# Fewer, larger transfers through a new row layout, and a new order of the stages of each quad, in a fused attention and ternary feed-forward kernel

## The chip, the cores and the metric

One core of one Trainium2 chip runs the whole kernel. The metric is the device time of one execution in microseconds (us). Everything stated of the hardware below comes from one profiled execution of the kernel before and from three timed ones.

## The reference, cut to what matters

```python
x = x + layernorm(attention(layernorm(x)))            # x: 8 x 1024 x 256, float32
x = x + layernorm(layernorm(x) @ (ternary(W) * alpha).T + bias)

# attention: 16 heads of 16, clipped relative positions (64 each way)
logits = einsum('bhqd,bhkd->bhqk', q, k) + einsum('bhqd,qkd->bhqk', q, embK[idx])
w      = softmax(logits)
out    = einsum('bhqk,bhkd->bhqd', w, v) + einsum('bhqk,qkd->bhqd', w, embV[idx])
return out @ Wo.T + bo

# ternary: delta = 0.7 * mean|w|;  +1 above delta, -1 below -delta, else 0
```

The mask is all ones and isn't used. The softmax subtracts the row's largest logit.

## The kernel before, in words

The work is 128 **steps**: 8 batches, 2 groups of 8 heads each, 8 query tiles of 128 tokens. Four steps are a **quad**, so a batch is four quads. A quad's slots in the planner's table are 32 long.

Queries and keys are split into three bfloat16 parts, and a logit is the sum of six products of parts over the 16 channels, which is one contraction over 96 rows. To these rows come two rows that carry minus the row's maximum (`MAXROW`) and three that carry the relative term of far keys (`FAR`): 101 rows in the tiles `qs` (queries) and `ks` (keys). The parts travel through DRAM (`qd`, `kd`), since each channel has to move to another partition: `write_q`, `write_k` and `write_far` (L643, L713) store them, `load_q`, `load_k` (L772, L722) bring them back in rows. A second, smaller copy for the row maxima, `mqs` and `mks` (48 main rows and 3 far rows, two heads on two halves of the partitions), comes by `load_mq` and `load_mk` (L751, L731).

One step issues on TensorE (the planner's stage names, with the letters used below):

- `row_max` (S, L919): main products of the *next* steps' queries into one of three banks `scores`; VectorE reduces each to a maximum (L1216, L1222).
- `max_rows` (L929): turns the maxima; SyncE moves them into `qs` (`max_move`, L812).
- `band_raw` (L902): the relative logits of near keys against `bandtab`; ScalarE copies them to `praw` (L1403, L1404), SyncE writes them skewed to DRAM `bs` (`band_write`, L785) and reads them back as `bands` (`band_read`, L798).
- `weights`: logits of one key tile for four heads, in one of two banks `logitsT`. A **plain block** (P) is four matmuls (L946). A **near block** (N), two of the eight per head group, adds four matmuls of `bands` (L946 and L950 in turn). ScalarE takes the exponential of each block out of its bank (L1424) into `wl`, `wm`, `wr` or `wy`. A step has 16 blocks. A block waits on `exp_ready` until its bank, that of the block before the last, was read.
- `weighted` (V): weights times values into `oacc` (L970), in kind X (the first four key tiles) and Y (the other four).
- once a quad: `relative` (L982), `relative_sum` (L995), `out_norm` (L1006); once a tile of the second group the **tail**: `tail_attT`, `tail_x1T` (L1020), `tail_wo`, `tail_ff` (L1034), with VectorE and GpSimd around them; once per two tiles of the next batch the **chunk**: `turn_x` (L865), `project_q`/`project_k` (L875), `far` (L883), `project_v` (L892).

The order of all of it is not written as code. `PLACES` (L109 to L169) gives each stage a slot within its quad, `LAG` and `END_LAG` shift a stage on one engine, `HOLD` says how long a stage keeps one of the two `misc` banks; `timetable()` lays the slots out, `with_banks` puts off what finds no bank, `order_of` sorts each engine's stages by slot. Engines then run these lists with semaphore waits. Four of TensorE's slots per half step are `near` (the blocks X0 to X3), four `rest` (Y0 to Y3). SyncE issues all DMAs, in its list's order.

The start of the program is special: batch 0's four chunks (256 tokens each) are projected, stored and loaded before the first step; in front of the list come constant loads (L656 to L661), fills of constant rows by DMA from a tile `junk` (L668, L672) and from zeros (L677). `load_table` (L689, L692) brings the tables of the later stages, at slots -33.2 on. `ternary` (L856 and VectorE) makes the ternary weight from `wf`.

## Time and profile before

| what | value |
|---|---|
| timed runs | 2567.48, 2572.11, 2575.16 us, median 2572.11 |
| profiled execution, span from first to last instruction | 2568.1 us |
| profiled execution, its own time | not listed beside the span |
| mean granted TensorE clock | 0.979 of full speed |
| TensorE matmul busy (PE) | 2413.4 us, 94% |
| VectorE busy (DVE) | 2072.1 us, 81% |
| ScalarE busy (ACT) | 1564.0 us, 61% |
| GpSimd busy (POOL) | 955.9 us, 37% |
| DMA queue of SyncE | 695686 packets, 427.75 MB, 60.8% of 16 engines' span |

PE is TensorE's matmuls, PEld its weight loads, which overlap them. A window row gives busy time with the number of instructions for each engine, then the granted clock, the DMA engines' busy share and GB/s. A timeline row gives the start, the length, and in brackets the idle time in front of it with what ended it; several equal instructions in a row are one row with a count. A row of SPq is a DMA issue on SyncE's queue: its length is the time of issuing, not of the transfer.

### The profile page before, as it was taken

Reading aid. Unit: us, or ns where it says so; the run is one execution under the profiler, and the core shown is the slowest. Engines: PE = TensorE matmul, PEld = TensorE weight load, DVE = VectorE, ACT = ScalarE, POOL = GpSimd, SP = SyncE. Lnnn points to the kernel's source line nnn. Section 1 sums busy time; section 2 is a strip of 40 time slices with the busy share of each in tenths; the row PEclk is TensorE's granted clock in tenths of the full one; section 3 lists DMA queues with packets and bytes.
Section 4 is the critical chain, followed back from the end, with each engine's and each line's share of the span. In section 5 each row is a group of like instructions: output and inputs, shape, how many; then the busy total and the mean of one; then the engine's idle time right before and its main releaser. Section 6 shows DMA issues by size and latency. Waiting matters only on the chain.

```text
span 2568.1 us, 101028 instructions
## 1 busy us (share of the span) xinstructions
PE 2413.4 (94%) x41858; PEld 1747.5 (68%) x41858; DVE 2072.1 (81%) x5306; ACT 1564.0 (61%) x2993; POOL 955.9 (37%) x2211
## 2 busy tenths in 40 slices
PE   5499999999999999999999999999999999999995
PEld 4266776777766776767776677676776777676673
DVE  4477779877888878887788878987788877888876
ACT  2266666666666666666666666666666666666651
POOL 3001534435343354425444253433534335442024
PEclk8599999999999999999999999999999999999998
DMA  6856675666746576565756667566774657756510
GB/s 162 228 155 180 184 195 146 167 176 193 205 138 174 165 205 185 148 193 152 206 153 176 184 182 194 147 168 174 199 201 139 173 163 203 192 145 189 153 42 29
DMA packets 696145, 434.20 MB, mean 169 GB/s; under 512 B 215846, under 2 KB 695430, under 8 KB 695558
## 3 DMA queue, kind: packets, MB, share of 16 engines
q1 hardware_dynamic: 695686, 427.75, 60.8%
q8 instruction: 329, 5.39, 0.9%
q14 instruction: 130, 1.06, 0.1%
HBM read 231.91 MB, written 194.92 MB: 166 GB/s over the span
## 4 chain that ended last, share of the span: by engine, by line
PE 54%; DVE 13%; issue 4%; ACT 3%; POOL 1%; DMA 0%; SPq 0%; DVEq 0%; ACTq 0%; POOLq 0%
PE logitsT L946 13%; PE oacc L970 12%; PE scores L919 7%; PE logitsT L950 6%; DVE junk L1222 4%; DVE maxes L1216 4%; PE misc L1034 3%; PE misc L875 3%; PE misc L995 2%; PE misc L892 2%; PE misc L902 1%; ACT wr L1424 1%; PE misc L982 1%; DVE stats L1092 1%; PE misc L1006 1%
## 5 line engine op out<-in xcount | busy, mean ns | idle before, releaser
L946 PE MATMUL logitsT<-qs,ks 98*128 98x128 bf16 (+1 forms) x8192 | 915.7, 221 | 21.8 <-ACT wr L1424 8.8
L1222 DVE CUSTOM_DVE_ANT_1 junk<-scores,bands 128x512 bf16<-128x512 f32 x988 | 679.5, 688 | 216.1 <-PE scores L919 66.7
L1424 ACT ACTIVATE wy<-logitsT 128x512 f32<-128x512 f32 x1024 | 581.4, 597 | 332.3 <-PE logitsT L946 321.1
L946 PEld LDWEIGHTS logitsT<-qs,ks 98*128 98x128 bf16 (+1 forms) x8192 | 562.4, 99 | 274.9 <-issue 150.4
L1216 DVE TENSOR_REDUCE maxes<-scores 128x1 f32<-128x512 f32 x1024 | 656.5, 682 | 93.8 <-PE scores L919 92.5
L919 PE MATMUL scores<-mks,mqs 48*128 48x256 bf16 (+6 forms) x3712 | 448.5, 289 | 36.8 <-DVE maxes L1216 12.6
L1424 ACT ACTIVATE wr<-logitsT 128x512 f32<-128x512 f32 x512 | 305.3, 596 | 200.2 <-PE logitsT L946 191.6
L950 PE MATMUL logitsT<-ident,bands 128*128 128x128 f32 x2048 | 410.6, 278 | 0.0
L1453 POOL TENSOR_SCALAR rs<-rs 128x1 int32<-128x1 int32 (+1 forms) x217 | 48.6, 224 | 803.3 <-DVE rs L1097 793.8
L950 PEld LDWEIGHTS logitsT<-ident,bands 128*128 128x128 f32 x2048 | 293.2, 143 | 20.6
L1458 POOL TENSOR_SCALAR rs<-rs 128x1 f32<-128x1 f32 x744 | 282.7, 383 | 64.9
L970 PE MATMUL oacc<-wy,vs 128*17 128x128 f32 (+1 forms) x9216 | 275.2, 262 | 4.5 <-ACT wy L1424 4.0
L919 PEld LDWEIGHTS scores<-mks,mqs 48*128 48x128 bf16 (+1 forms) x3712 | 138.9, 94 | 196.9 <-DVE maxes L1222 30.2
L1424 ACT ACTIVATE wl<-logitsT 128x512 f32<-128x512 f32 x256 | 158.6, 619 | 154.3 <-PE logitsT L950 152.5
L1463 POOL TENSOR_SCALAR rs<-rs 128x1 f32<-128x1 f32 x744 | 219.6, 298 | 66.1
L970 PEld LDWEIGHTS oacc<-wy,vs 128*17 128x17 f32 x9216 | 206.2, 97 | 53.1 <-issue 34.7
L1403 ACT ACTIVATE praw<-misc 128x512 f32<-128x512 f32 x256 | 154.7, 604 | 40.3 <-DMA bs<-praw 32.5
L1245 DVE COPY_PREDICATED wm<-later,wl 128x512 f32<-128x512 int32 x224 | 171.1, 764 | 0.0
L1424 ACT ACTIVATE wm<-logitsT 128x512 f32<-128x512 f32 x256 | 152.9, 597 | 24.6 <-PE logitsT L950 3.8
L970 PE MATMUL oacc<-wr,vs 128*17 128x128 f32 (+1 forms) x4608 | 159.3, 261 | 0.0
L1404 ACT ACTIVATE praw<-misc 128x512 f32<-128x512 f32 x256 | 157.5, 615 | 0.0
L902 PE MATMUL misc<-bandtab,qs 96*128 96x128 bf16 x1024 | 100.3, 220 | 20.3 <-ACT praw L1404 14.5
(147 smaller groups left out, 2991.3 us busy)
## 6 DMA issues: line engine op xcount, KB each, us to landing
bs<-praw SPq DMA_DIRECT2D x256, 512.0 KB, 4.6
bands<-bs SPq DMA_DIRECT2D x224, 512.0 KB, 4.5
ks<-kd SPq DMA_DIRECT2D x64, 384.0 KB, 4.9
qs<-qd SPq DMA_DIRECT2D x112, 192.0 KB
bands<-bs SPq DMA_DIRECT2D x128, 128.0 KB, 3.3
mks<-kd SPq DMA_DIRECT2D x128, 96.0 KB, 3.8
qd<-qparts SPq DMA_DIRECT2D x60, 192.0 KB, 2.6
kd<-kparts SPq DMA_DIRECT2D x60, 192.0 KB, 2.6
```

The source lines that it names most:

```text
L919: mm = e.matmul(scores[(u + side) % NSCORE][:, c % 512:c % 512 + length], mqs[i][HALF * side:HALF * side + depth, p, :], kk[HALF * side:HA ...
L946: mm = e.matmul(lt[:, j * P:(j + 1) * P], kk[0:depth, SLOT[HB * blk + j], kt * P:(kt + 1) * P], qs[i][0:depth, SLOT[HB * blk + j], :], sta ...
L950: mm = e.matmul(lt[:, j * P:(j + 1) * P], band[v % BRING][:, j, c * P:(c + 1) * P], ident[:], start=False, stop=True, is_transpose=True, s ...
L970: mm = e.matmul(oacc[32 * j:32 * j + VW, o0 + q0:o0 + q1], vs[m_ % VRING][:, int(right), kt, h, :], src, start=first and c == 0, stop=True ...
L1216: e.tensor_reduce(top, sc[:], AX.X, ALU.max).then_inc(row_maxed, 1)
L1222: e.tensor_tensor_reduce(junk[:], sc[:].rearrange("p (a c) -> p a c", a=2), banded, 1.0, LOWEST, ALU.add, ALU.max, top).then_inc(row_maxed, 1)
L1245: e.copy_predicated(right, mask.bitcast(I32), left).then_inc(merged, 1)
L1403: e.activation(dst[:, :, 0:P], src, ACT.Copy)
L1404: e.activation(dst[:, :, P:WIN], src[:, :, P - 1:P].broadcast_to([P, HB, P]), ACT.Copy).then_inc(praw_ready, 1)
L1424: e.activation(dst, src, ACT.Exp).then_inc(exp_ready, 1)
L1458: op = e.tensor_scalar(rs[k][:, 3, x:x + 1], rs[k][:, 2, x:x + 1], rs[k][:, 0, x:x + 1], rs[k][:, 2, x:x + 1], ALU.mult, ALU.mult)
L1463: op = e.tensor_scalar(rs[k][:, 2, x:x + 1], rs[k][:, 3, x:x + 1], 1.5, rs[k][:, 2, x:x + 1], ALU.add, ALU.mult)
```

## The change

**Layout.** The rows of `qs` and `ks` are reordered: the two maximum rows are 0 and 1, the parts 2 to 97, the far rows 98 to 100. `QPARTS` is now (1, 0, 2, 0, 1, 0) and `KPARTS` (1, 2, 0, 0, 0, 1), `MAIN` is 3*D, so that the 48 main rows lie against the far rows and one transfer brings both. DRAM `qd` has 99 rows, `kd` is laid out with both groups of a chunk side by side. The constants come in fewer, merged arrays (`firsts`, `wkv`, `bvf`, `emb`, `wof`, `bof`, `rels`), some on ScalarE's queue. The constant rows are set by GpSimd with memsets over whole tiles (`ks`, `mks`, two rows of each `qs`) before its list begins. `band_raw` contracts 98 rows instead of 96 (two of them times zero).

DMAs of one call, before and after: `load_q` 2 to 1, `load_mq` 4 to 2, at query tile 0 `load_q` 4 to 3 and `load_mq` 8 to 6, `write_q` 6 to 5, `write_k` 6 to 3, constants 11 to 6, embedding tables 4 to 1, later tables 8 to 4, fills 6 to 0, zeroing of `qd` 4 to 0. Of 2646 DMA issues on SyncE, 2104 are left, and 8 stand on ScalarE.

**Order.** New numbers in `PLACES`, `LAG`, `HOLD`. The cut diff:

```diff
-QPARTS = (0, 0, 0, 1, 1, 2)
-KPARTS = (2, 0, 1, 0, 1, 0)
-MAIN = D
+QPARTS = (1, 0, 2, 0, 1, 0)
+KPARTS = (1, 2, 0, 0, 0, 1)
+MAIN = 3 * D
...
-MAXROW = SPLIT
-FAR = MAXROW + 2
+MAXROW = 0
+PART0 = 2
+FAR = PART0 + SPLIT
...
+ 'load_table': (-20.0, 3.085, 5.0, 7.0, 9.0),
+ 'ternary': 17.535,
...
- 'near': (0.0, 0.76, 0.72, 0.98),
- 'rest': (1.76, 2.1, 2.5, 2.77),
+ 'near': (0.0, 0.76, 0.075, 0.687),
+ 'rest': (1.735, 1.699, 2.423, 2.671),
  'value_x': 2.3,
- 'value_y': 4.12,
+ 'value_y': 3.809,
...
-    for i in range(9):
-        at(-33.2 + i, "load_table", i)
...
-    at(-93.9, "clear_bands")
-    at(4, "ternary")
...
 LAG = ...
-         'out_norm': 0.7,
-         'tail_wo': 0.7,
+         'out_norm': 0.003,
+         'tail_wo': 0.127,
...
-        qd = [nc.dram_tensor(f"qd{i}", [G, ROWS, HG, S], BF16).ap() for i in range(2)]
+        qd = [nc.dram_tensor(f"qd{i}", [G, DROWS, HG, S], BF16).ap() for i in range(2)]
-        kd = [nc.dram_tensor(f"kd{i}", [G, SPLIT, HG, S], BF16).ap() for i in range(2)]
+        kd = [nc.dram_tensor(f"kd{i}", [SPLIT, HG, NCHUNK, G, CT], BF16).ap() for i in range(2)]
...
+            for t_ in ks:
+                e.memset(t_[:].rearrange("r h s -> r (h s)").bitcast(F32), TWO_ONES).then_inc(k_ones_set, 1)
+            for t_ in qs:
+                op = e.memset(t_[MAXROW:PART0].rearrange("r h c -> r (h c)").bitcast(F32), 0.0)
+            op.then_inc(q_rows_set, 1)
+            for t_ in mks:
+                e.memset(t_[:].rearrange("r h s -> r (h s)").bitcast(F32), TWO_ONES).then_inc(mk_ones_set, 1)
```

What that does to the lists is seen in three places.

**TensorE, in step 39, around V of kind X**: `scores` rows are S, a pair of rows `logitsT<-qs,ks` a plain block, with `bands` a near block, `oacc` is V. Before:

```order
L946 MATMUL logitsT<-qs,ks 128x128 [waits exp_ready]
L946 MATMUL logitsT<-qs,ks 128x128 x3
L946 MATMUL logitsT<-qs,ks 128x128 [waits exp_ready]
L946 MATMUL logitsT<-qs,ks 128x128 x3
L919 MATMUL scores<-mks,mqs 128x128 [waits row_maxed] x2
L919 MATMUL scores<-mks,mqs 128x128 x2
L919 MATMUL scores<-mks,mqs 128x256 x2
L946 MATMUL logitsT<-qs,ks 128x128 [waits exp_ready]
L946 MATMUL logitsT<-qs,ks 128x128 x3
L970 MATMUL oacc<-wl,vs 17x128 x4
L970 MATMUL oacc<-wm,vs 17x128 x4
L970 MATMUL oacc<-wr,vs 17x128 x8
```

After:

```order
L955 MATMUL logitsT<-qs,ks 128x128 [waits exp_ready]
L955 MATMUL logitsT<-qs,ks 128x128 x3
L955 MATMUL logitsT<-qs,ks 128x128 [waits exp_ready]
L955 MATMUL logitsT<-qs,ks 128x128 x3
L928 MATMUL scores<-mks,mqs 128x128 [waits row_maxed] x2
L928 MATMUL scores<-mks,mqs 128x128 x2
L928 MATMUL scores<-mks,mqs 128x256 x2
L979 MATMUL oacc<-wl,vs 17x128 x4
L979 MATMUL oacc<-wm,vs 17x128 x4
L979 MATMUL oacc<-wr,vs 17x128 x8
L955 MATMUL logitsT<-qs,ks 128x128 [waits exp_ready]
L955 MATMUL logitsT<-qs,ks 128x128 x3
```

The plain block that stood alone between S and V is gone from there and follows V, next to another plain block.

**TensorE, step 40, the end of a near block and what follows.** Before:

```order
L950 MATMUL logitsT<-ident,bands 128x128
L946 MATMUL logitsT<-qs,ks 128x128
L950 MATMUL logitsT<-ident,bands 128x128
L946 MATMUL logitsT<-qs,ks 128x128 [waits exp_ready]
L946 MATMUL logitsT<-qs,ks 128x128 x3
L919 MATMUL scores<-mks,mqs 128x256 [waits row_maxed,mks_in1_0,mqs_in1]
L919 MATMUL scores<-mks,mqs 128x256 [waits row_maxed]
L919 MATMUL scores<-mks,mqs 128x256 [waits mks_in1_1]
L919 MATMUL scores<-mks,mqs 128x256
L946 MATMUL logitsT<-qs,ks 128x128 [waits exp_ready]
L946 MATMUL logitsT<-qs,ks 128x128 x3
L946 MATMUL logitsT<-qs,ks 128x128 [waits exp_ready]
```

After:

```order
L959 MATMUL logitsT<-ident,bands 128x128
L955 MATMUL logitsT<-qs,ks 128x128
L959 MATMUL logitsT<-ident,bands 128x128
L928 MATMUL scores<-mks,mqs 128x256 [waits row_maxed,mks_in1_0,mqs_in1]
L928 MATMUL scores<-mks,mqs 128x256 [waits row_maxed]
L928 MATMUL scores<-mks,mqs 128x256 [waits mks_in1_1]
L928 MATMUL scores<-mks,mqs 128x256
L955 MATMUL logitsT<-qs,ks 128x128 [waits exp_ready]
L955 MATMUL logitsT<-qs,ks 128x128 x3
L955 MATMUL logitsT<-qs,ks 128x128 [waits exp_ready]
L955 MATMUL logitsT<-qs,ks 128x128 x3
```

The plain block that stood between the near block and S is now ahead of the near block, so that the near block is followed by S and then by two plain blocks. Of places where a near block, one S and two plain blocks follow each other with nothing between, the old order has 54 and the new one 119. Of places where a plain block stands after S and is followed by S again (P, S, P), there were 251 and there is 1. Places where a plain block directly follows a near block go from 88 to 257. Sorting the matmuls of TensorE's list into three classes (S alone; V, `relative`, `relative_sum` and `far`, which write 32 rows each to their own part of a bank; all others), neighbours of different classes occur 2942 times in the old order and 2796 times in the new one.

**SyncE, the last transfers before the first step.** Before:

```order
L687 DMA rd<-relout 128x32 [waits rel_ext_ready]
L689 DMA later<-in_later 128x128
L689 DMA relsel<-in_relsel 128x128
L689 DMA relmask<-in_relmask 128x2
L689 DMA wf<-in_WfT 128x2x256
L689 DMA wo<-in_WoT 128x2x256
L689 DMA bo<-in_bo 128x256
L689 DMA bf<-in_bf 128x256
L689 DMA alpha<-in_alpha 128x1
L692 DMA reltab<-rd 128x2048 [waits rel_ext_out]
L785 DMA bs<-praw 128x4x256 [waits praw_ready] x2
L798 DMA bands<-bs 128x4x256 [waits band_out2]
```

After:

```order
L726 DMA qd<-oT 8x3x128 [waits far_ready]
L726 DMA qd<-oT 8x3x128 x3
L693 DMA rd<-relout 128x32 [waits rel_ext_ready]
L695 DMA later<-in_later 128x128
L793 DMA bs<-praw 128x4x256 [waits praw_ready] x2
L806 DMA bands<-bs 128x4x256 [waits band_out2]
L806 DMA bands<-bs 128x4x256 [waits band_out3]
```

The tables of the later stages (`wof`, `bof`, `rels` and `reltab`) have gone from here to behind the first steps' band writes and reads, 17 to 24 rows further on; `rd` and `later` have stayed.

## Rows read from the trace of the kernel before

**Rows 1.** The page's part 1 (busy us, share, instructions), and the window 200:2480.
```profile
PE 2413.4 (94%) x41858; PEld 1747.5 (68%) x41858; DVE 2072.1 (81%) x5306; ACT 1564.0 (61%) x2993; POOL 955.9 (37%) x2211
...
200.00:2480.00 2280.00, 2219.28 (x39323) 1614.37 (x39321) 1893.85 (x4821) 1458.16 (x2783) 891.63 (x2027) 1.00 0.63 174
```

**Rows 2.** Windows, first and last quad of one batch's four: PE, PEld, DVE, ACT, POOL.
```profile
1021.00:1102.00 81.00, 78.84 (x1342) 56.61 (x1338) 73.32 (x195) 50.33 (x95) 35.11 (x99) 1.00 0.55 156
...
1255.00:1326.00 71.00, 69.33 (x1266) 50.61 (x1264) 60.61 (x160) 46.05 (x88) 28.48 (x70) 1.00 0.67 180
```

**Rows 3.** Timeline of PE near 1005 us.
```profile
1005.29 0.39 PE L946 MATMUL logitsT<-qs,ks 101*128 101x128 bf16 x4
1005.52 0.39 PE L902 MATMUL misc<-bandtab,qs 96*128 96x128 bf16 x4
1005.84 0.39 PE L919 MATMUL scores<-mks,mqs 48*128 48x256 bf16 x4
1006.16 0.23 PE L946 MATMUL logitsT<-qs,ks 101*128 101x128 bf16 x1
```

**Rows 4.** Timeline of PEld after a near block, at 360 and at 1011 us.
```profile
360.22 0.23 PEld L946 LDWEIGHTS logitsT<-qs,ks 98*128 98x128 bf16 x4 [0.23 <-issue]
360.65 0.23 PEld L946 LDWEIGHTS logitsT<-qs,ks 98*128 98x128 bf16 x4 [0.21 <-ACT wm L1424]
...
1010.94 0.23 PEld L946 LDWEIGHTS logitsT<-qs,ks 101*128 101x128 bf16 x4 [0.18 <-ACT wr L1424]
1011.27 0.12 PEld L919 LDWEIGHTS scores<-mks,mqs 48*128 48x128 bf16 x4
1011.64 0.23 PEld L946 LDWEIGHTS logitsT<-qs,ks 101*128 101x128 bf16 x4 [0.25 <-ACT wm L1424]
```

**Rows 5.** Waits of PEld, 200:2480: us in total, times, longest.
```profile
PEld logitsT L946 <- ACT wr L1424: 54.9, 226, 0.4
PEld scores L919 <- DVE maxes L1216: 25.6, 71, 1.0
PEld logitsT L946 <- ACT wm L1424: 21.8, 96, 0.3
```

**Rows 6.** Timeline of PE in the start.
```profile
82.61 0.61 PE L919 MATMUL scores<-mks,mqs 51*128 51x512 bf16 x2 [10.72 <-DMA mks<-kd]
...
99.56 0.59 PE L902 MATMUL misc<-bandtab,qs 96*128 96x128 bf16 x4 [10.64 <-ACT praw L1404]
...
113.19 0.29 PE L946 MATMUL logitsT<-qs,ks 98*128 98x128 bf16 x1
...
127.06 0.59 PE L856 MATMUL misc<-small,ybuf 128*128 128x1 f32 x2 [2.68 <-DVE small L1156]
```

**Rows 7.** Timeline of ACT in the start.
```profile
98.33 0.60 ACT L1403 ACTIVATE praw<-misc 128x512 f32<-128x512 f32 x1 [24.90 <-DMA bs<-praw]
```

**Rows 8.** Timeline of SPq, the issues ahead of and at the band writes.
```profile
86.85 0.47 SPq L689 DMA_DIRECT2D wo<-in_WoT  x1
...
88.83 0.43 SPq L692 DMA_DIRECT2D reltab<-rd  x1
89.30 1.27 SPq L785 DMA_DIRECT2D bs<-praw  x2
```

**Rows 9.** The page's part 6, and a window of the start.
```profile
bs<-praw SPq DMA_DIRECT2D x256, 512.0 KB, 4.6
...
80.00:90.00 10.00, 5.38 (x18) 1.34 (x18) 6.74 (x16) 0.00 (x0) 0.00 (x0) 0.50 1.03 263
```

**Rows 10.** Timeline of POOL at the beginning.
```profile
0.73 0.31 POOL L1470 MEMSET bands<- 128x256 f32 x1 [0.29 <-POOLq L1555]
...
13.76 0.19 POOL L1453 TENSOR_SCALAR rs<-rs 128x2 int32<-128x2 int32 x1 [11.39 <-DVE rs L1097]
```

**Rows 11.** The page's part 3 (packets, MB, share of 16 engines), and the fullest 20 us window.
```profile
q1 hardware_dynamic: 695686, 427.75, 60.8%
...
1220.00:1240.00 20.00, 19.97 (x309) 14.46 (x311) 14.24 (x35) 14.69 (x31) 11.23 (x22) 1.00 0.92 244
```

More of the change, by code:

```diff
@@ L132 @@
- 'first_load_mk': (-83.13, -73.03, -63.03, -62.73),
- 'load_mk': (-41.8, -33.7, -25.7, -17.91),
- 'load_mq': -21.5,
- 'first_load_mq': (-83.18, -73.73, -61.06, -50.13),
- 'load_q': -32.7,
+ 'load_k': (-41.8, -33.8, -25.8, -17.939),
+ 'first_load_mk': (-83.13, -73.441, -63.218, -62.73),
+ 'load_mk': (-41.8, -33.7, -24.33, -20.033),
+ 'load_mq': -22.727,
+ 'first_load_mq': (-83.554, -73.717, -61.06, -50.13),
+ 'load_q': -33.822,
  'raw': (-28.8, -25.4),
  'band_write': (-26.51, -22.8),
- 'band_read': (-22.18, -20.26),
@@ L151 @@
- 'piece_by': 0.37,
+ 'relative': (29.57, 31.51),
+ 'piece_by': 0.313,
  'sum': (33.44, 34.25),
- 'norm': (35.47, 36.59),
+ 'norm': (35.369, 36.59),
  'tail': 38.0,
  'tail_by': 8.0,
- 'tail_late_by': 6.5,
+ 'tail_late_by': 6.428,
  'tail_load': -1.0,
- 'tail_attT': -0.28,
- 'tail_wo': 1.0,
- 'tail_x1': 3.0,
- 'tail_norm': 3.5,
+ 'tail_attT': -0.821,
+ 'tail_wo': 1.037,
+ 'tail_x1': 3.115,
+ 'tail_norm': 4.469,
  'tail_normed': 5.5,
- 'tail_x1T': 10.15,
+ 'tail_x1T': 10.101,
  'tail_ff': 11.3,
@@ L166 @@
  'tail_store': 15.82,
- 'end': 36.6,
+ 'end': 36.637,
  'end_by': 0.66,
@@ L177, in at @@
         slots.append((slot, stage, k))
-    at(-60, "write_reltab")
-    for i in range(9):
-        at(-33.2 + i, "load_table", i)
+    at(x_["write_reltab"], "write_reltab")
+    for i in range(5):
+        at(x_["load_table"][i], "load_table", i)
     at(-98.5, "tables")
     at(-102.1, "far_table")
-    at(-93.9, "clear_bands")
-    at(4, "ternary")
+    at(x_["ternary"], "ternary")
     chunk_stages = ("turn_x", "project_q", "far", "project_k", "project_v", "write_q", "write_far", "write_k")
@@ L312 @@
          'tail_out': 1.9},
- 'ACT': {'turn_x': -0.23, 'far': 0.4, 'project_q': 1.2, 'band_raw': -0.13},
+ 'ACT': {'turn_x': -0.23, 'far': 0.146, 'project_q': 0.615, 'band_raw': -0.13},
  'POOL': {'project_q': 3.4,
-          'project_k': 2.0,
+          'project_k': 1.916,
           'far': 2.0,
-          'tail_wo': 1.8,
+          'tail_wo': 2.621,
           'tail_x1': 1.1,
@@ L359 @@
             "tail_wo": "lin_ready", "tail_ff": "lin_ready", "ternary": "threshold_ready"}
-HOLD = {'turn_x': 0.06,
- 'project_q': 1.25,
+HOLD = {'turn_x': -0.44,
+ 'project_q': 0.662,
  'project_k': 0.92,
- 'far': 0.45,
+ 'far': -0.183,
  'project_v': 0.45,
- 'band_raw': 0.2,
+ 'band_raw': 0.151,
  'max_rows': 0.23,
@@ L610, in q_loads @@
         def q_loads(s):
-            return 32 * sum(1 if tile_of(x) else 2 for x in range(s % QRING, s + 1, QRING))
+            return 16 * sum(1 if tile_of(x) else 3 for x in range(s % QRING, s + 1, QRING))
         def mq_loads(s):
-            return 64 * sum(1 if tile_of(x) else 2 for x in range(s % MRING, s + 1, MRING))
+            return 32 * sum(1 if tile_of(x) else 3 for x in range(s % MRING, s + 1, MRING))
         def last_scored(s):
@@ L635, in wait_chunk_loaded, with runs_of, write_queries, write_keys @@
                     eng.wait_ge(ks_in[nn % 2][c], 16 * (nn // 2 + 1))
[L637 removed]
+        def runs_of(parts):
             for k in range(3):
                 at_ = [r for r in range(NB) if parts[r] == k]
[L641 to L645 removed]
+                yield k, at_[0], at_[1] - at_[0] if len(at_) > 1 else 1, len(at_)
+        def write_queries(e, b, c, qp, done):
+            for k, first, step, times in runs_of(QPARTS):
+                at_ = first * D * HG * S + c * CT
+                if times == 1:
+                    e.dma_start(bass.AP(qd[b % 2].tensor, at_, [[S, P], [DROWS * HG * S, G], [1, CT]]), qp[:, k]).then_inc(done, 16)
+                    continue
+                for g in range(G):
+                    e.dma_start(bass.AP(qd[b % 2].tensor, g * DROWS * HG * S + at_, [[S, P], [step * D * HG * S, times], [1, CT]]),
+                                qp[:, k, g:g + 1, :].broadcast_to([P, times, CT])).then_inc(done, 16)
+        def write_keys(e, b, c, kp, done):
+            for k, first, step, times in runs_of(KPARTS):
+                e.dma_start(bass.AP(kd[b % 2].tensor, (first * D * HG * NCHUNK + c) * G * CT,
+                                    [[G * S, P], [step * D * HG * G * S, times], [1, G * CT]]),
+                            kp[:, k:k + 1].rearrange("p k g t -> p k (g t)").broadcast_to([P, times, G * CT])).then_inc(done, 16)
+        def keys_of(b, g, c, rows, slots):
+            return bass.AP(kd[b % 2].tensor, ((rows.start * HG + slots.start) * NCHUNK + c) * G * CT + g * CT,
+                           [[HG * G * S, rows.stop - rows.start], [G * S, slots.stop - slots.start], [1, CT]])
+        def no_far(heads):
+            return zeros[0:ROWS - FAR, 0:heads * HALF // 2].bitcast(BF16).rearrange("r (h c) -> r h c", h=heads)
         def sync_program(e):
@@ L871, in tensor_program @@
                     pe.wait_ge(*free)
[L872 removed]
+                    pe.wait_ge(wq_in if stage == "project_q" else wkv_in, 16)
                     for g in range(G):
```

278 lines of the change are left out of this document (133 added, 145 removed).

## The prediction

> **What bounds it now.** I read the page's busy times first: TensorE's matmuls fill 94% of the span, VectorE 81% [rows 1]. Between 200 and 2480 us they fill 2219.3 of 2280 us at the full clock [rows 1], so 61 us at most are idle there; the rest is work, and a busy matmul row is not all work, since rows overlap and contain short waits. The windows of the quads say it again: 78.8 of 81 us in the longest quad of a batch, 69.3 of 71 in the shortest [rows 2]. In steady state only what TensorE executes, or waits for between two groups, counts. Two such costs are to be seen.
>
> The first is the change between kinds of matmul. Four matmuls L946 take 0.23 us from start to start when L902 follows (1005.29 to 1005.52). Four L902 followed by L919 take 0.32, and four L919 followed by L946 take 0.32 as well [rows 3], although all are short matmuls of 128 to 256 columns. So I read 0.09 us for a change of class, in either direction.
>
> The second is the bank of `logitsT`. A plain block lasts 0.23 us, an exponential 0.60. At 360.22 and 360.65 us two plain blocks follow S behind a near block: the second begins 0.43 us after the first, with 0.21 of waiting for the exponential of the near block [rows 4]. Over the 2280 us the loads of L946 waited for `wr` and `wm` 76.7 us, 322 times [rows 5].
>
> The start is bounded otherwise. The first near block begins at 113.19 us [rows 6]. Before it TensorE idles 10.72 us for `mks` and 10.64 for `praw` [rows 6]; ScalarE could not fill `praw` until 98.33, since it waited for the band writes `bs<-praw` [rows 7]. These were issued at 89.30, right behind ten issues of the table loads, the last `reltab` [rows 8], and took 9.0 us to land where the median is 4.6 [rows 9]; the DMA engines were full in 80:90 [rows 9].
>
> **The change, part by part.**
>
> *Tables out of the start.* Ten issues stood ahead of `bs`, two remain. Eight issues of 0.43 to 0.47 us [rows 8] are 3.6 us off SyncE's queue. With 1 MB of `reltab` and the weights no longer in the engines, the band write should land in the median 4.6 us instead of 9.0, which is 4.4 more. Together 8.0: `praw` is free at about 90.3, and all behind it moves by as much. The tables come later, between band transfers of the first steps; their first user is `relative`, 29.6 slots behind the quad's beginning, and `ternary`, moved from slot 4 to 17.5. A quad of 32 slots lasts some 76 us (mean of [rows 2]), a slot 2.4, so the tables have over 40 us: cost nothing, and if that cover were gone, `relative` would wait for part of their transfer, at most 8 us. The 2.68 us for `small` [rows 6] go with `ternary`'s move; behind that stall the first blocks were late anyway, so I count 1.
>
> *Fills by GpSimd.* The memsets are 14,848 columns of 32 bits a partition (twice 4096, five times 512, twice 2048). At 0.31 us for 256 [rows 10] that is 18 us. GpSimd was idle until 13.76 [rows 10], so about 7 us come too late for its first roots of the variance, and after them for the far rows. The fills by DMA that go away held SyncE's queue in the same stretch. Bounds: nothing, if the first chunk (which VectorE does alone) carries the beginning, and +6. It is nearest to nothing, as TensorE waits for later things than this, [rows 6]; I take 1. Start in all: -8.0 - 1 + 1 = **-8** (bounds -14, if writes of keys and queries, which lose four issues a chunk, bring the last chunk forward too, and -2).
>
> *Fewer DMAs in steady state.* 542 issues fewer on SyncE. The DMA engines' mean share is 0.61, and in the fullest stretch, at 0.92, TensorE was still busy 19.97 of 20 us [rows 11]: fewer issues and as many bytes change nothing for it, so nothing. Contracting 98 rows instead of 96 costs nothing either: `logitsT` with 98 and with 101 rows has the same lengths in [rows 4].
>
> The Trainium skill speaks against this part: its page "DMA: Bandwidth & Descriptors", section "Why a DMA increments its semaphore by 16 and not by 1", says that a transfer goes over the largest number of engines, up to 16, that divides its slowest dimension, and over the lowest-numbered ones. By that rule loads of 51 and 99 rows would use 3 and 11 engines, and the sum would end at the last rival's 2581 instead; no row here shows the rule at work.
>
> *Changes of class.* 2942 - 2796 = 146 fewer, by 0.09 us: **-13**. They lie on TensorE, which is the path, so all of it counts where nothing else is late: bounds -13 and 0.
>
> *Pairs of plain blocks.* N, S, P, P rises from 54 places to 119: 65 by 0.21 [rows 4] is +13.7. Against that, the 251 places P, S, P vanish. Such a place stands at 1010.94 to 1011.64, with 0.25 of waiting behind S [rows 4]. Were all like it, 63 us would go, which is nearly all of the 76.7 waited in the window, so the bound is far. I take the mean share: 76.7 us over some 1,820 blocks of that window (2048 in all) is 0.042 a block, by 250 is -10.5. A third place, a plain block directly behind a near block, rises by 169; the one row of it has 0.18 [rows 4], but there a plain block also stood directly ahead of the near block, and in the new order mostly `band_raw` does: nothing, with 30 us as the bound. Net +3, of bounds -40 and +44.
>
> *Lags of the tails, the end of the program*: hundredths to tenths of a slot, on engines that are not the path until the last tiles: nothing, 2 us either way.
>
> Sum: -8 - 13 + 3 = -18, of the profiled span: 2568.1 becomes 2550. The span lies 4 us under the median of the runs, 2572.1, which becomes **2554**.
>
> **Rivals.**
>
> *The new pairs are no new waits.* The row at 1011.64 waits for `wm` too, in the old pattern N, P, S, P. If the second block behind a near block waits in both orders, the +13.7 falls away: 2540. For it speaks that 96 times or more `wm` was not ready. Chance 0.22.
>
> *Only the start pays.* VectorE has 73.3 of 81 us in the long quads [rows 2], and the loads of L919 wait for its maxima 25.6 us [rows 5]. What TensorE saves in classes, it then waits for the next bank of `scores`. Steady state comes out even: 2564. Against it: the short quads have 10 us of VectorE's time free [rows 2]. Chance 0.22.
>
> *The layout does not do what it says.* The start is held by the late GpSimd as by the tables before, and the rest is even: 2572. Chance 0.05.
>
> *The exponentials bind.* The slower side in one mechanism: the 169 added places N, P each pay the 0.18 of [rows 4], as the block just ahead of the near one is still with ScalarE. That is +30, so 2584. It decides from 18/169 = 0.11 us a place. Against it stands ScalarE's 61% busy [rows 1]. Chance 0.05.
>
> *Lopsided transfers.* The loads of queries now have 99 and 51 rows and don't divide over 16 engines as 96 and 48 did. If the two `load_mq` of a step (204 packets each) went over 3 engines and the `load_q` (792) over 11, the most loaded engines would get 68 + 68 + 72 = 208 packets a step instead of 72. A packet takes 0.036 us (60.8% of 16 engines' 2568 us, over 695,686 [rows 11]), so 136 more are 4.9 us of a step's 19: a quarter of those engines' time. In the fullest stretch, at 0.92 [rows 11], they would then lack 0.17 x 20 = 3.4 us, and bands would come late once a batch and more: 8 x 3.4 = +27, 2581. Against it: a band is read some 20 slots ahead of its use. It decides when a backlog outlasts these 48 us. Chance 0.05. This is the case of the rule cited above, of the Trainium skill's page "DMA: Bandwidth & Descriptors".
>
> **How the numbers follow.** Forecast 2554: 0.41 (its own range 2546 to 2562). With the rivals at 2540, 2564, 2572, 2584 and 2581: 0.22, 0.22, 0.05, 0.05, 0.05. A measurement of this kernel tells about 0.3%, 7.7 us, from no change, so faster is under 2564.4: 0.41, 0.22 and half of 0.22, and a little of the third rival's, 0.75. Same: 0.16. Slower: 0.09. The range goes from 2530, as 2540 may carry more of the vanished waits (bound -40), to 2574, past the case of no gain: what lies outside is the slower side and a tail below.
>
> **What would show it.** Right: the first near block at about 105 us instead of 113, `bs<-praw` landing in under 6 us at the time of the second step, no wait for `small`. In steady state quads of 80 and 70 us instead of 81 and 71, `wm` waits more often than 96 times, `wr` less often than 226. Wrong: waits of L919 for the maxima grow by over 10 us (only the start pays); TensorE's loads wait for `bands` or `qs` by DMA (lopsided); the start's near block at 113 or later with GpSimd busy ahead of it.

## The result, and the profile after

The changed kernel takes **2488.1 us** (median of 4 runs, 2486.8 to 2489.0), the kernel before 2573.5 in the same comparison (4 runs, 2567.5 to 2575.2). The ratio is 0.9675, with a 95% interval of 0.966 to 0.969. That is 85 us less where 18 were forecast, and far outside the range of 2530 to 2574. The direction was right and the size was not.

The page of the changed kernel answers to [rows 1] and [rows 11]:

```profile
span 2487.2 us, 100503 instructions
PE 2360.2 (95%) x41858; PEld 1743.2 (70%) x41858; DVE 2072.3 (83%) x5306; ACT 1533.3 (62%) x2993; POOL 955.0 (38%) x2219
...
q1 hardware_dynamic: 655632, 424.52, 58.7%
```

As many matmuls as before are busy 53 us less. Their rows contain short waits and changes of class, and part of those went, as the waits of the weight loads below show.

**Where the 81 us of span went.** I cut both traces at the 128 instructions `misc<-ident,negmax` (one a step). The stretch from the 9th to the 125th, 29 quads, lasts 2199.6 us before and 2136.0 after: **63.6 us, in steady state**. Up to the 9th it is 241.7 and 229.0: 12.7 in the start. From the 125th to the end it is 126.8 and 122.2: 4.6. Sum 80.9. The windows of one batch's quads, cut at the same instructions, before and then after (columns as in [rows 2], whose windows had the right lengths but stood across the edges of the quads):

```profile
852.00:933.00 81.00, 79.43 (x1357) 58.82 (x1355) 61.26 (x149) 51.90 (x104) 43.47 (x75) 1.00 0.63 177
933.00:1011.90 78.90, 76.88 (x1321) 56.68 (x1318) 65.53 (x166) 49.12 (x95) 30.34 (x64) 1.00 0.72 195
1011.90:1086.90 75.00, 73.18 (x1306) 52.62 (x1303) 67.57 (x182) 47.54 (x91) 32.58 (x92) 1.00 0.53 148
1086.90:1157.80 70.90, 67.83 (x1264) 48.33 (x1261) 59.97 (x155) 45.87 (x86) 20.99 (x61) 1.00 0.65 181
```

```profile
821.50:899.50 78.00, 77.54 (x1358) 58.82 (x1356) 60.97 (x149) 51.26 (x104) 43.46 (x79) 1.00 0.65 190
899.50:975.30 75.80, 75.14 (x1320) 56.44 (x1317) 64.30 (x166) 48.13 (x95) 29.54 (x62) 1.00 0.67 197
975.30:1049.20 73.90, 71.84 (x1306) 52.70 (x1302) 67.35 (x182) 46.55 (x91) 32.18 (x93) 1.00 0.53 155
1049.20:1117.40 68.20, 66.75 (x1263) 48.56 (x1261) 59.69 (x155) 44.56 (x86) 20.12 (x58) 1.00 0.63 181
```

Every quad is shorter, by 1.1 to 3.1 us, and the weight loads (the second busy time of a row) are the same. VectorE is busy 61.3 of 81.0 us in the longest quad and 67.6 of 75.0 in the third, and not 73.3 of 81, as the window of [rows 2] had it.

The waits of PEld over those 29 quads, before and then after, answer to [rows 5] (total us, times, longest; `issue` is time for which the profile shows no cause):

```profile
PEld logitsT L946 <- issue: 136.0, 625, 0.5
PEld logitsT L946 <- ACT wr L1424: 52.6, 216, 0.4
PEld scores L919 <- DVE maxes L1216: 24.5, 68, 1.0
PEld scores L919 <- DVE maxes L1222: 21.3, 52, 1.3
PEld logitsT L946 <- ACT wm L1424: 20.3, 89, 0.3
```

```profile
PEld logitsT L955 <- issue: 86.0, 402, 0.2
PEld logitsT L955 <- ACT wm L1445: 19.7, 96, 0.2
PEld logitsT L955 <- ACT wr L1445: 15.3, 71, 0.2
PEld scores L928 <- DVE maxes L1231: 13.1, 45, 0.8
PEld scores L928 <- DVE maxes L1225: 10.8, 42, 0.4
```

The waits for `wr` fall by 37 us, those for the maxima from 45.8 to 23.9, those for `wm` stay.

Where in the order did the waits for exponentials stand? I sorted the first weight load of every block by its neighbours, each block into the first kind that fits, over the same 29 quads (waited: for an exponential):

| kind of place | before: places, waited, us | after: places, waited, us |
|---|---|---|
| plain block directly behind a near block (N, P) | 80, 80, 14.7 | 232, 0, 0 |
| plain block behind P, S (P, S, P) | 228, 68, 15.4 | none left |
| second plain block of N, S, P, P | 45, 45, 9.3 | 104, 96, 19.7 |
| plain block directly ahead of V | 99, 87, 25.7 | 21, 0, 0 |
| other plain blocks | 940, 38, 10.3 | 1035, 100, 21.6 |
| near blocks | 464, 30, 8.2 | 464, 31, 8.1 |

So the 37 us of `wr` are not those of P, S, P, where only 1.9 us of the 15.4 were waits for `wr` and 11.0 were for `wm`. They are those of N, P (14.6) and of the last plain block ahead of V (25.7), less what came back at other plain blocks. A block of N, P stands in [rows 4] at 1010.94 us. The other two kinds follow each other here in the kernel before, P, S, P at 1070.25 and the block ahead of V at 1070.74:

```profile
1069.89 0.11 PEld L919 LDWEIGHTS scores<-mks,mqs 48*128 48x128 bf16 x4
1070.25 0.23 PEld L946 LDWEIGHTS logitsT<-qs,ks 101*128 101x128 bf16 x4 [0.24 <-ACT wm L1424]
1070.74 0.23 PEld L946 LDWEIGHTS logitsT<-qs,ks 101*128 101x128 bf16 x4 [0.26 <-ACT wr L1424]
1071.07 0.13 PEld L970 LDWEIGHTS oacc<-wl,vs 128*17 128x17 f32 x8
```

The pair of plain blocks behind N and S is there as the forecast had it, with its 0.20 us:

```profile
974.27 0.12 PEld L928 LDWEIGHTS scores<-mks,mqs 48*128 48x128 bf16 x4
974.60 0.23 PEld L955 LDWEIGHTS logitsT<-qs,ks 101*128 101x128 bf16 x4 [0.21 <-issue]
975.03 0.23 PEld L955 LDWEIGHTS logitsT<-qs,ks 101*128 101x128 bf16 x4 [0.20 <-ACT wm L1445]
```

**The start** answers to [rows 6]:

```profile
16.28 1.11 PE L873 MATMUL misc<-ident,wm 128*128 128x128 f32 x4 [16.28 <-DVE wm L1051]
...
85.53 0.61 PE L928 MATMUL scores<-mks,mqs 51*128 51x512 bf16 x2 [10.81 <-DMA mks<-kd]
...
94.02 0.59 PE L911 MATMUL misc<-bandtab,qs 98*128 98x128 bf16 x4 [2.18 <-ACT praw L1423]
...
108.41 0.29 PE L955 MATMUL logitsT<-qs,ks 98*128 98x128 bf16 x1
```

The wait for `praw` fell from 10.64 to 2.18 us, nearly as forecast. The way was another: the band write was issued at 89.74 us, no earlier than before (89.30), and landed 3.0 us later instead of 9.0. All of it came from the transfer and nothing from the shorter queue, since what stands ahead in the queue ran later. But everything up to the wait for `mks` came later than before (85.53 against 82.61), and TensorE began at 16.28 instead of 8.61. VectorE, which does the first chunk alone, and GpSimd show why:

```profile
5.24 3.55 DVE L1106 TENSOR_SCALAR rs<-mv 128x2 f32<-128x2 f32 x1
8.82 4.04 DVE L1115 TENSOR_SCALAR rs<-rs 128x2 int32<-128x2 int32 x1
```

```profile
1.75 7.02 POOL L1497 MEMSET ks<- 101x4096 f32 x2
8.70 2.39 POOL L1499 MEMSET qs<- 2x512 f32 x5
11.04 3.56 POOL L1502 MEMSET mks<- 128x2048 f32 x2
```

The same two instructions took 0.17 us each before. In the changed kernel the first lies beside the second fill of `ks` (5.25 to 8.77 us), the second beside the five short fills of `qs` and the first fill of `mks`, six instructions in a row (8.70 to 12.84). Each ends when these end. That was in none of my terms. Not every VectorE instruction was held:

```profile
4.02 0.75 DVE L1101 BATCH_NORM_STATS2 stats<-wm 128x6 f32<-128x256 f32 x2 [2.62 <-DMA wm<-in_x]
12.90 0.46 DVE L1120 TENSOR_SCALAR rs<-rs 128x1 f32<-128x1 f32 x2
```

The first pair runs beside the first fill of `ks`, the second beside the second fill of `mks` (12.79 to 14.60), and both take what they take without a fill.

### The profile page after: what moved, and what is told of

Same layout as the page of the kernel before. It is cut to its first block, busy times and chain, and to the rows that moved or that the text cites. A ratio compares the mean times of both kernels' runs of the same rounds, so it can differ in the third digit from the quotient of the medians.

```text
span 2487.2 us, 100503 instructions
## 1 busy us (share of the span) xinstructions
PE 2360.2 (95%) x41858; PEld 1743.2 (70%) x41858; DVE 2072.3 (83%) x5306; ACT 1533.3 (62%) x2993; POOL 955.0 (38%) x2219
## 4 chain that ended last, share of the span: by engine, by line
PE 67%; DVE 23%; issue 6%; SPq 2%; ACT 1%; POOL 1%; DMA 1%; DVEq 0%; POOLq 0%; ACTq 0%
PE logitsT L955 16%; PE oacc L979 14%; PE scores L928 10%; DVE junk L1231 7%; PE logitsT L959 7%; DVE maxes L1225 7%; PE misc L883 5%; PE misc L1004 2%; PE misc L991 2%; PE misc L1043 2%; PE misc L900 2%; PE misc L911 2%; DVE stats L1101 2%; PE misc L1015 1%; DVE mv L1104 1%
## 5 line engine op out<-in xcount | busy, mean ns | idle before, releaser
L955 PE MATMUL logitsT<-qs,ks 98*128 98x128 bf16 (+1 forms) x8192 | 878.4, 221 | 7.6 <-ACT wy L1445 3.0
L1445 ACT ACTIVATE wy<-logitsT 128x512 f32<-128x512 f32 x1024 | 561.6, 596 | 375.0 <-PE logitsT L955 367.7
L1225 DVE TENSOR_REDUCE maxes<-scores 128x1 f32<-128x512 f32 x1024 | 656.6, 682 | 81.8 <-PE scores L928 79.2
L955 PEld LDWEIGHTS logitsT<-qs,ks 98*128 98x128 bf16 (+1 forms) x8192 | 582.9, 99 | 183.5 <-issue 96.4
L1445 ACT ACTIVATE wr<-logitsT 128x512 f32<-128x512 f32 x512 | 314.3, 614 | 127.8 <-PE logitsT L955 126.3
L1479 POOL TENSOR_SCALAR rs<-rs 128x1 f32<-128x1 f32 x744 | 279.2, 378 | 64.9
L1484 POOL TENSOR_SCALAR rs<-rs 128x1 f32<-128x1 f32 x744 | 211.7, 287 | 66.1
L1254 DVE COPY_PREDICATED wm<-later,wl 128x512 f32<-128x512 int32 x224 | 177.3, 791 | 0.0
L1043 PE MATMUL misc<-wof,rowsT 128*128 128x256 f32 x512 | 144.9, 406 | 6.0 <-ACT rowsT L1458 3.3
```

Source lines behind the costliest of these rows:

```text
L955: mm = e.matmul(lt[:, j * P:(j + 1) * P], kk[0:depth, SLOT[HB * blk + j], kt * P:(kt + 1) * P], qs[i][0:depth, SLOT[HB * blk + j], :], sta ...
L1043: mm = e.matmul(m[:, 0:H], rowsT[:, ih, :], w[:, ih, :], start=ih == 0, stop=ih == 1)
L1225: e.tensor_reduce(top, sc[:], AX.X, ALU.max).then_inc(row_maxed, 1)
L1254: e.copy_predicated(right, mask.bitcast(I32), left).then_inc(merged, 1)
L1445: e.activation(dst, src, ACT.Exp).then_inc(exp_ready, 1)
L1479: op = e.tensor_scalar(rs[k][:, 3, x:x + 1], rs[k][:, 2, x:x + 1], rs[k][:, 0, x:x + 1], rs[k][:, 2, x:x + 1], ALU.mult, ALU.mult)
```

## The experiments

All are timed beside the kernel before, whose medians in the four groups of runs were 2570.8, 2571.7, 2569.2 and 2571.4 us. Where two experiments of different groups are compared, a difference of some us is read with that in mind.

### Layout or order?

**The layout alone**: the changed kernel with every old number.

```diff
- 'near': (0.0, 0.76, 0.075, 0.687), ... (all new numbers)
+ 'near': (0.0, 0.76, 0.72, 0.98), ... (all old numbers; tables from slot -33.2 on, ternary at 4)
```

> The changed kernel's layout with all old numbers of the order (tables loaded early, ternary at slot 4). Theory (the steady gain of 64 us is the order's, the layout gives none there): 2570 to 2580 us, quads of 81, 78, 75 and 71 us as before, and the start at most 3 us different. Rival (fewer transfers carry the gain): under 2530 us, with the short quads of the changed kernel.

Measured 2566.1 us, ratio 0.9981 (0.9972 to 0.9991), which is under the 2570 to 2580 that I expected. The quads are 81, 78, 75 and 71 us: nothing in steady state (2198.9 us against 2199.6), and 5 us in the start up to the 9th maxima turned, where I had allowed 3.

**The order alone**: the kernel before with every new number except `load_table` and `ternary`.

> The kernel before with all new numbers of the order, except for the table loads and ternary, which stay where they were. Theory (order carries the steady gain): about 2573 - 64 = 2509 us, 2502 to 2516, with quads of 78, 76, 74 and 68 us. Rival (layout carries it): over 2550 us.

Measured 2513.2, ratio 0.9772 (0.9756 to 0.9787): 58 us are the order's, 54 of them in the 29 quads of steady state (2145.8 us). The changed kernel's 2136.0 is 10 us less still, although the layout alone gave nothing there: the two parts are worth more together. One quad in four is longer than in the changed kernel (76.5 to 79.2 us against 75.8 to 76.4), with waits for the move of the maxima, `DMA qs<-nm`, of 7.4 us in all, which the changed kernel doesn't have. That these waits went because the layout's queue on SyncE is shorter fits the traces, but no run shows it by itself; the kernel before had no such waits, so the layout alone had none to take.

**Tables early**: the changed kernel with

```diff
- 'load_table': (-20.0, 3.085, 5.0, 7.0, 9.0), 'ternary': 17.535,
+ 'load_table': (-33.2, -30.2, -28.2, -32.2, -25.2), 'ternary': 4,
```

> The changed kernel with the table loads back ahead of the first steps and ternary at slot 4. Theory (the wait for the band writes comes back): 2488 + 8 = 2496 us, 2493 to 2501, and about 9 us of idle ahead of the second band_raw at 90 to 100 us. Rival (the start is bound by the keys' chain and the tables had room): 2488 +- 2.

Measured 2499.7, 12 us slower than the change (10 us by the spans of the two traces), with 9.46 us of waiting for `praw` ahead of the second `band_raw`, as expected. The first turned maximum comes 5.3 us later (103.5 against 98.2), the fifth 9.8 later. The band write is issued at the same time in both, 89.75 and 89.74 us, and lands 8.3 us later instead of 3.0: these are the 5.3. The rest lies between the second and the third maximum turned, 20.0 us instead of 14.4. There TensorE waits 1.48 us for `small` (at 127.16) and 1.80 for the maxima, and its granted clock, which had risen to full at 122.9, is at half (1.2 instead of 2.4 GHz) once more from 133.2 to 136.6, where the changed kernel has the full clock from 117.0 on. By the clock's share of the two stretches that is 2.2 us. My sum had neither this nor the waits.

### Which part of the order?

Each of these is the kernel before with some of the new numbers. "Blocks" are `near`, `rest` and `value_y`; "scores" `row_max`, `max_reduce` and `band_read`; "tails" `relative`, `norm` and the tails; "loads" `load_q`, `load_mq`, `load_k`, `load_mk`.

```diff
- 'near': (0.0, 0.76, 0.72, 0.98), 'rest': (1.76, 2.1, 2.5, 2.77), 'value_y': 4.12,
+ 'near': (0.0, 0.76, 0.075, 0.687), 'rest': (1.735, 1.699, 2.423, 2.671), 'value_y': 3.809,
```

> The kernel before with only the places of the eight blocks and of V of kind Y (near, rest, value_y) from the change. Theory (changes of class, 12 us, and the waits of blocks for the exponentials, 36 us in the two traces, are all of this part, while 18 us of waits of S for VectorE's maxima come from other moves): about 2525 us, 2518 to 2535. First rival (these places carry everything in steady state): 2505 to 2515. Second rival (they carry little without the other moves): over 2550.

> The kernel before with the new places of the blocks and of V, and also the new places of row_max, max_reduce and band_read (fractions of a slot). Changes of class fall from 2889 to 2820 against the blocks alone, 69 x 0.09 = 6 us. Theory (S and the blocks are tuned to each other; most of the 39 us between the blocks alone, 2552, and the whole order, 2513, is here, with the waits of S for VectorE's maxima, 43 to 23 us): 2520 to 2530. Rival (only the changes of class count): 2543 to 2548, waits for maxima still over 38 us.

> The kernel before with the new places of the blocks and of V, and the new places of relative, norm and the tails. Changes of class 2889 to 2865, 2 us. Theory (scores and blocks carry the rest): 2545 to 2552. Rival (the tails free VectorE at the right time, so the waits for maxima go): 2525 to 2538.

> The kernel before with every new number of the order except near, rest and value_y. If the parts add up, 58 - 19 = 39 us of gain remain: 2533. Theory (the other numbers pay only together with the blocks): 2555 to 2575, with waits for wr still near 50 us and changes of class at 2914. Rival (independent parts): 2528 to 2538.

One more difference stands in these kernels. X1 is the last block of the near slots in the new order, so in the kernels with "blocks" in their name, in "all but scores" and in the two further down (with the loads, with the lags) the band read waits for X1 instead of X3 before it fills a buffer again; "all but blocks", "all" and the changed kernel still wait for X3. In the traces of "blocks, scores", "blocks, scores, tails" and "all" SyncE never stood still for a block ahead of a band read. In that of "blocks" it did so 14 times and in the kernel before 13. What this edit alone does was not tried.

| new numbers of | us | ratio (95%) | changes of class | wr | maxima |
|---|---|---|---|---|---|
| none | 2571 | 1 | 2942 | 50 | 45 |
| blocks | 2551.8 | 0.9921 (0.9907 to 0.9936) | 2889 | 15 | 43 |
| blocks, scores | 2548.1 | 0.9912 (0.9887 to 0.9937) | 2820 | 19 | 34 |
| blocks, tails | 2539.8 | 0.9884 (0.9855 to 0.9914) | 2865 | 17 | 35 |
| blocks, scores, tails | 2530.6 | 0.9849 (0.9833 to 0.9865) | 2796 | 17 | 24 |
| all but blocks | 2557.6 | 0.9941 (0.9921 to 0.9962) | 2914 | 58 | 45 |
| all but scores | 2529.5 | 0.9834 (0.9816 to 0.9852) | 2865 | 16 | 31 |
| all | 2513.2 | 0.9772 (0.9756 to 0.9787) | 2796 | 16 | 23 |

(The last two columns are waits of PEld in us, over the 28 quads from the 9th maxima turned to the 121st, in the trace of each.)

The waits for `wr` go with the blocks and with nothing else: 50 to 15 us by them alone, 58 without them. By kind of place, over 29 quads: with the blocks alone N, P and the blocks ahead of V wait nothing; in all but the blocks they wait 25.4 and 25.7 us. The blocks alone are worth 19 us of time, though 35 us of waits for `wr` went, since others came: idle time ahead of V, `band_raw` and the tails' matmuls grew, in the same trace, and all waits of PEld together fell only from 433 to 425 us. My expectation of 2525 for the blocks was a miss, because it took a fall of waits for a fall of time. So were those of 2520 to 2530 for blocks and scores (2548.1) and of 2545 to 2552 for blocks and tails (2539.8, between theory and rival). The classes and the waits for maxima belong to blocks, scores and tails together.

> The kernel before with the new places of the blocks and V, of row_max, max_reduce and band_read, and of relative, norm and the tails; lags, holds, chunk, loads and first chunks as before. Changes of class are 2796, as in the whole new order. Theory (the three parts are tuned to each other, and with all three the gain of the whole order is there): 2510 to 2520, quads of 78, 76 to 77, 74 and 68 us, waits for maxima near 23 us. Rival (lags and holds or loads are needed too): 2528 to 2540.

> The kernel before with the whole new order except row_max, max_reduce and band_read. Changes of class 2865 instead of 2796, 69 x 0.09 = 6 us. Theory (only with the scores moved by fractions of a slot do the waits for maxima fall): 2525 to 2540, waits for maxima over 35 us. Rival (only the classes): 2517 to 2522, waits for maxima near 23 us.

The three together gave 39 of the 58 us and all of the fall in the waits for maxima. Its expectation of 2510 to 2520 missed: 17 us were elsewhere. The scores are worth nothing clear beside the blocks alone (2548.1 against 2551.8), and 16 us beside everything else (2529.5 against 2513.2), more than the 6 us of their classes. Without them I expected the waits for maxima over 35 us, and they were 31, so part of that fall doesn't need them.

> The kernel before with the new places of blocks, scores and tails, and the new places of load_q, load_mq, load_k and load_mk (load_q and load_mq about 1.1 slots earlier). Theory (the missing part is queries that arrive late: waits for qs by DMA of 12.7 us in the three parts alone): those waits fall under 2 us and the time from 2530.6 to 2517 to 2523. Rival (lags and holds): 2528 to 2532.

Measured 2549.8, ratio 0.9902 (0.9876 to 0.9928), **19 us slower** than without the loads. The waits for late queries did go (0.0 us), those for maxima rose from 24 to 45 us, and one quad in four went from about 79 to 83 or 84 us. The timelines of SPq and DVE at such a place:

```profile
887.91 2.17 SPq L738 DMA_DIRECT2D mqs<-qd  x4
890.12 1.38 SPq L799 DMA_DIRECT2D qs<-nm  x2
891.54 0.44 SPq L683 DMA_DIRECT2D xc<-in_x  x1
```

```profile
889.64 1.29 DVE L1203 TENSOR_REDUCE maxes<-scores 128x1 f32<-128x512 f32 x2 [0.99 <-PE scores L906]
894.64 0.75 DVE L1079 BATCH_NORM_STATS2 stats<-xc 128x6 f32<-128x256 f32 x2 [3.71 <-DMA xc<-in_x]
...
896.00 0.69 DVE L1209 CUSTOM_DVE_ANT_1 junk<-scores,bands 128x512 bf16<-128x512 f32 x1
```

The earlier loads stand ahead of `load_x` in SyncE's queue, whose slot was left where it was. The next chunk's x comes late, VectorE stands still for 3.71 us in front of its statistics, the maxima behind it come late, and TensorE waits for them. Seven such waits of VectorE sum to 27.6 us. The windows of the same place show that TensorE's granted clock fell to half behind it:

```profile
889.00:896.00 7.00, 5.34 (x76) 3.74 (x74) 2.54 (x7) 3.98 (x10) 2.92 (x3) 1.00 0.61 165
...
898.60:902.00 3.40, 3.40 (x48) 2.48 (x44) 2.08 (x6) 2.09 (x5) 3.05 (x9) 0.50 1.13 345
```

Such a stretch of 3.4 us at half the clock stands 2 to 4 us behind each of the seven, and there are two more; the kernel without the loads has none between 140 and 2470 us. Nine of them cost at most 15 us at the clock's share. The whole order has `load_x` 1.8 slots earlier as well, and none of this. That `load_x` is the cause is read from these rows; no run moved it alone.

> The kernel before with the new places of blocks, scores and tails, and all new LAG, END_LAG and HOLD. Theory (late queries are the larger part): 2524 to 2530. Rival (lags and bank holds are the missing part): 2513 to 2519, with waits for qs by DMA still over 8 us or gone as a consequence of a different order of band_raw.

Measured 2517.1, ratio 0.9773 (0.9747 to 0.9798): with the lags and bank holds nearly all of the order's gain is there. The waits for queries stay (18.8 us), so the theory of late queries was wrong as the cause of the 17 us: lags and holds are worth 13 of them by the medians and all of them by the ratios (0.9773 against 0.9849 and, for the whole order, 0.9772). Which of the lags or holds it is was not tried.

### The fills

```diff
-            for t_ in ks:
-                e.memset(...ks...).then_inc(k_ones_set, 1)
...
+            pool.wait_ge(xn_ready[0], 1)      # VectorE has normalised chunk 0
+            fill(ks[0], k_ones_set)
+            fill(mks[0], mk_ones_set)
...
+                    if done == NCHUNK - 1:    # the last far rows of batch 0
+                        fill(ks[1], k_ones_set)
+                        fill(mks[1], mk_ones_set)
```

> The changed kernel with the four big memsets moved: ks and mks of the first group behind VectorE's first normalisation, those of the second group behind the last far rows of batch 0; what is set stays the same. In the changed kernel's trace two VectorE instructions that took 0.17 us before took 3.55 and 4.04 us while GpSimd filled ks (1.75 to 8.77 us), and TensorE began at 16.28 instead of 8.61. Theory (the memset holds VectorE up): both take 0.17 again, TensorE begins at about 9, first near block 3 to 7 us earlier, 2481 to 2485 us. Rival (the fills or VectorE's waits have another cause, or the start is bound elsewhere): 2488 +- 2.

Measured **2481.0 us** (4 runs, 2479.0 to 2485.4), ratio to before 0.9651 (0.9627 to 0.9675), so 7 us faster than the change by the medians. The intervals of the two ratios overlap a little, but the start of the trace shows the same 7 us. TensorE began at 9.07, the first near block at 101.04 instead of 108.41. The timeline of DVE, with GpSimd's next fill of `ks` at 9.07 to 12.59:

```profile
5.29 0.17 DVE L1106 TENSOR_SCALAR rs<-mv 128x2 f32<-128x2 f32 x1
5.49 0.17 DVE L1115 TENSOR_SCALAR rs<-rs 128x2 int32<-128x2 int32 x1
...
10.14 2.47 DVE L1106 TENSOR_SCALAR rs<-mv 128x2 f32<-128x2 f32 x1
```

Both instructions are back to 0.17 us, and the same instruction for the next chunk now takes 2.47, ending with the fill that it met. This shows that the fill holds these VectorE instructions up. The Trainium skill's page "SBUF — State Buffer", section "Terms", has the rule: the two engines arbitrate for one pair of ports, the lock is exclusive and held for the whole instruction, and the loser blocks. The 3.55 and 2.47 us agree. The 4.04 us are longer than one instruction of GpSimd: six fills in a row passed first. And the rows above with 0.75 and 0.46 us beside a fill show that not every instruction of VectorE loses. I had not weighed this rule: it spoke against the part of the change that I costed at 1 us. (The expectation above puts both held instructions beside the fills of `ks`; the second was beside those of `qs` and `mks`.)

### The rule of the divisor

> The kernel with the later fills (2481.0 us), its loads of 51 and 99 rows each cut into two, of 48 and 3 or 96 and 3 rows; three issues more a step, same bytes. In its start four L764 issues take 4.1 us and two L782 3.4 us. Theory (the layout's fewer issues are neutral to helpful, engines are not lopsided enough to matter): 2481 to 2487, the start no earlier. Rival (51 and 99 rows load a few DMA engines with most packets, and SyncE's queue backs up): the first near block 3 us or more earlier than 101.0, 2473 to 2478 us.

```diff
-    e.dma_start(mqs[i][r0:r0 + MDEPTH], src[MAIN:DROWS, ...])
+    for lo, hi in ((0, MROWS), (MROWS, MDEPTH)):
+        e.dma_start(mqs[i][r0 + lo:r0 + hi], src[MAIN + lo:MAIN + hi, ...])
```

Measured 2480.8, the same as the 2481.0 of the kernel with later fills. The first near block came 2.6 us earlier (98.46) and the 9th maxima turned 3.5, against my expectation of a start no earlier. The 29 quads then took 2.4 us more (2137.4 us against 2135.0; most quads are the same to some tenths, one is 1.2 longer), and the stretch from the 125th to the end 2.6 more (124.2 against 121.6).

> The kernel with the later fills (2481.0 us), only the first five query loads and the first three maxima loads cut into 96 or 48 and 3 rows; all later ones have 99 and 51 rows. Theory (uneven engines cost in the start alone, where the DMA engines are full): first near block near 98.5 us instead of 101.0 and 2477.5 to 2479.5 us. Rival (the start's 2.6 us are given back anyway): 2480 to 2482.

Measured 2479.6 (2479.2 to 2480.1), ratio to before 0.9636 (0.9619 to 0.9652): 1.4 us under the later fills alone, which the runs can't tell from nothing. It is the fastest kernel of the study. The first turned maximum comes 3.7 us earlier (87.5 against 91.2), and most of it is given back: the 29 quads take 3 us more, one of them 79.2 instead of 78.0, and the end is 2 us longer. So loads of 99 and 51 rows cost some 3 to 4 us of the start, where the DMA engines' share is 0.80 to 0.94 (60 to 100 us, in the kernel with the later fills), and nothing of the kernel's time that these runs can tell. The rival that made them the loss of the kernel is out. Over how many engines such a load goes is not in these traces.

## Why the prediction was wrong, point by point

The sum failed in steady state: it had -10 us there and the traces show -64. Three of its steps failed. It priced two kinds of places at nothing that held 40 us of waits (blocks behind N, and blocks ahead of V); it had no term for the waits for the maxima; and it put lags at nothing and had no term for the holds.

- **What bounds it**: right. TensorE was the path, by what it executes and by short waits. I had said that the 61 us of open idle time were not the limit of what could go, but the sum still went as if they were: over 28 quads the weight loads waited 433 us before and 384 after, in time that looks busy.
- **Tables out of the start, -8 and -1**: `praw` waited until 92.79 instead of 98.33, which is 5.5 us; undoing it costs 12. The half that was the landing was right and too small (6.0 us against 4.4). The half that was the queue, 3.6, did not show, since the band write was issued no earlier. The lower clock behind the tables was missing. I had also said that no wait for `small` would be left: 0.83 us are, at 146 us, where `ternary` now stands. The start up to the 9th maxima turned gained 12.7 us in all.
- **Fills by GpSimd, +1**: wrong. They took 13 us, not 18, but their price was not their length: two VectorE instructions were held for 7.2 us. Moving the fills gave 7.1 us back.
- **Changes of class, -13**: consistent with the traces. I took the lower quartile of the time from one matmul's start to the next one's for each pair of kinds, in both traces together; by these prices the changed kernel's neighbours cost 11.6 us less over 28 quads, in which 126 changes went (0.09 each), and those of blocks, scores and tails, with the same 2796 changes, 11.5. No run moved classes alone.
- **Pairs, +13.7**: right place by place and beside the point in sum. The second blocks of N, S, P, P wait 10.4 us more in 29 quads. But the places P, S, P had 11.0 us of waits for `wm` too, and those went, so that the count for `wm` stays at 89 before and 96 after. In sum this was my first rival, at 0.22.
- **P, S, P, -10.5**: of about the right size. These are the places where S stands between two plain blocks. 68 of 228 waited, 15.4 us in all, and none is left. The row at 1011.64, with its 0.25, is one of the 68; had I gone by that row alone, I would have had 63 us, four times too much. That the mean of all blocks came so near was partly luck.
- **N, P, nothing**: wrong. I asked what the 169 added places would pay, and they pay nothing, as I said. I did not ask what the 88 old ones had paid: in 29 quads all 80 waited, 14.7 us, and that went. A plain block stood ahead of the near block in every one of them, and in 2 of the 257 new ones.
- **Blocks ahead of V, no term**: the largest single item. 87 of 99 waited, 25.7 us in 29 quads, and that went; in the new order the block ahead of V is mostly one that directly follows a near block. The runs with the blocks alone and with all but the blocks show that it goes with their places. Waits are not time, however: all of the blocks' new places together gave 19 us.
- **Waits of S for the maxima**: no term of mine; my rival had them grow. They fell by 22 us, when blocks, scores and tails were all moved; scores and tails beside the blocks brought some 20 us of time, classes included.
- **Lags, nothing**: wrong. With the three parts in place, lags and holds are worth at least 13 us.
- **Fewer DMAs in steady state, nothing**: right alone (layout: 5 us, all in the start). Beside the new order the layout brings 10 us more in steady state, with 7 us of waits for the maxima's move gone.
- **The rivals**: "only the start pays" is out by 63.6 us in steady state; it leant on VectorE's 73.3 of 81 us, a window across two quads, where the quad itself has 61.3. "The exponentials bind" is out, as none of the 232 places N, P waited; lopsided transfers are out by split_rows, and the layout's failing by layout_only and the result.
- **The range**: it added terms that I took near their middle, and its lower end left out the bounds of two of them (-40 for the blocks alone) although the text had them. Counting the waits of each kind of place in the trace before (14.7, 15.4 and 25.7 us off, some 10 on) instead of one row or one mean would have given about 2505, below my range. That is still 17 us above the result, and it would have been partly luck, as waits that go are not all time.

## What to carry to other kernels

Where an engine is 94% busy by its rows, the rows themselves hide waits: list the waits of its weight loads by what ended them and by their neighbours in the order, and count for each kind of place how many wait and how long, those that the new order removes as well as those that it adds. One row of a kind misleads as much as the mean of all does. Then take the sum as a bound: 35 us of waits gone were 19 us of time. Parts of an order are not worth what they bring alone: the loads of queries, 1.1 slots earlier, cost 19 us, by the traces because the load behind them in the queue was not moved too. A fill that replaces a few small transfers is not free on an idle engine if another engine, one that the start waits for, is held up meanwhile, here for 7.2 us.

## What the runs showed of the hardware that I had not expected

- A GpSimd memset of 4096 columns (3.51 us) held a small `TENSOR_SCALAR` of VectorE (128x2, 0.17 us without it) for 3.55 us, and six shorter memsets in a row held the next one for 4.04, to the end of the last. Two `BATCH_NORM_STATS2` at 4.02 us took their usual 0.75 together beside the same kind of fill, and `TENSOR_SCALAR` of 128x1 their usual 0.46.
- Behind one late load of x (3.71 us of idle VectorE, TensorE busy 5.34 of 7 us) TensorE's granted clock was 0.50 for 3.4 us in the middle of steady state, and so behind all seven of them; the changed kernel has 1.00 throughout its quads from 117 us on.
- A band write of 512 KB landed after 3.0 us without the table loads ahead of it and after 8.3 with them, though it was issued at the same time.
